# One-hot groups of an edge walk built from a row of numbers in PSUM in place of SBUF

## The reference

```python
xn = layernorm(x)
neigh_mean = segment_sum(xn[src], dst) / max(deg, 1)
gnn = normalize(relu(concat([xn, neigh_mean]) @ W + b))
mix = linear_attention(rmsnorm(xn))          # 4 heads, softmax of k over all nodes
x = x + gnn + mix
x = x + experts(layernorm(x))                # 8 experts of 256x1024x256, the best 2 of each row
```

## Time and profile before

| what | value |
|---|---|
| timed runs, median of 3 (lowest to highest) | 1980.42 us (1979.69 to 1981.53) |
| profiled execution: its span, from first to last instruction | 2187.4 us |
| time around that span | not on the page |
| PE, VectorE, ScalarE, GpSimd: busy in the span | 72%, 50%, 41%, 52% |
| the walk's first and last gather (L695) begin at | 89.5 and 1271.2 us |
| expert stage, from about 1500 us to the end: PE busy | 675 of 687 us |

### The profile page before, as it was taken

The page is one execution under the profiler, slowest core; times in us unless marked ns, Lnnn a source line. Parts: engine busy times, 40 slices in busy tenths (PEclk is TensorE's granted clock), DMA queues, the critical chain, the costliest instruction groups (busy, mean ns, idle before and its releaser), DMA issues.

```text
span 2187.4 us, 33907 instructions
## 1 busy us (share of the span) xinstructions
PE 1583.7 (72%) x9422; PEld 1361.2 (62%) x9423; DVE 1101.1 (50%) x3043; ACT 900.9 (41%) x1840; POOL 1140.4 (52%) x1141
## 2 busy tenths in 40 slices
PE   6735536546566667867767763548999999999998
PEld 5524435435454544545545543447999999999997
DVE  6512212212234536655555457765666666666664
ACT  6501101101112323323334336554666666666664
POOL 3267666666656666666666612555333333333333
PEclk9868868767878979988888785558999999999999
DMA  7334333333324655566656526537878777877775
GB/s 210 119 100 114 104 101 107 101 97 103 106 81 154 224 165 182 182 180 184 198 182 189 181 76 197 188 135 248 228 215 220 213 221 208 226 214 221 213 221 137
DMA packets 188123, 368.85 MB, mean 169 GB/s; under 512 B 33324, under 2 KB 134172, under 8 KB 173656
## 3 DMA queue, kind: packets, MB, share of 16 engines
q0 software_dynamic: 77296, 252.50, 41.3%
q1 hardware_dynamic: 102992, 113.64, 16.3%
q10 hardware_dynamic: 7736, 1.52, 0.4%
HBM read 287.94 MB, written 80.39 MB: 168 GB/s over the span
## 4 chain that ended last, share of the span: by engine, by line
PE 50%; another core or an unknown queue 17%; DVE 12%; issue 11%; DMA 5%; ACT 3%; SPq 2%; POOL 0%; DVEq 0%; ACTq 0%; POOLq 0%
PE bank L1813 11%; PE bank L2002 5%; PE bank L2003 5%; PE bank L2004 5%; PE bank L2025 5%; PE bank L2024 5%; PE bank L2026 5%; PE bank L1879 3%; DMA xTs<-xnT_d 3%; PE bank L1830 2%; PE bank L1973 1%; DVE acc_lent L1478 1%; DMA z_d<-w2s_lent 1%; DVE acc_lent L1307 1%
## 5 line engine op out<-in xcount | busy, mean ns | idle before, releaser
L695 POOL DMA_INDIRECT w2s_lent<-z_d,edge_tabs_lent x784 | 777.5, 992 | 438.7 <-issue 256.7
L1307 DVE TENSOR_TENSOR acc_lent<-acc_lent,bank 128x258 f32 x244 | 102.7, 421 | 600.6 <-remote 348.8
L1813 PE MATMUL bank<-w2s_lent,S_lent 128*128 x976 | 261.0, 416 | 19.0 <-issue 9.5
L1031 ACT ACTIVATE G<-bank,acc_lent 128x256 f32<-128x256 f32 x448 | 188.3, 472 | 205.9 <-DVE w2s L1670 124.5
L1813 PE MATMUL bank<-w2s_lent,G 128*128 x976 | 265.9, 422 | 3.4 <-issue 3.4
L2024 PE MATMUL bank<-w2s 128*128 128x256 f32 x896 | 264.4, 295 | 0.0
L2002 PE MATMUL bank<-w2s,acc 128*128 128x256 f32 x896 | 260.4, 291 | 2.8 <-issue 2.8
L739 POOL DMA_INDIRECT out_dram<-G,acc_lent x112 | 179.6, 1604 | 158.3 <-DVE G L1650 117.3
L1629 DVE TENSOR_TENSOR acc<-w1s,acc 128x512 fp32r<-128x512 f32 x224 | 155.1, 693 | 200.7 <-ACT acc L1000 174.1
L2004 PE MATMUL bank<-w2s,acc 128*128 128x256 f32 x896 | 254.0, 284 | 0.0
L2025 PE MATMUL bank<-w2s 128*128 128x256 f32 x896 | 253.7, 283 | 0.4 <-issue 0.4
(11 more groups left out here) (322 smaller groups left out, 2993.3 us busy)
## 6 DMA issues: line engine op xcount, KB each, us to landing
w2s<-w_d POOLq DMA_DIRECT2D x112, 1024.0 KB
w_d<-w2s_lent SPq DMA_DIRECT2D x64, 256.0 KB
acc_lent<-bucket_d SPq DMA_DIRECT2D x56, 266.0 KB
w2s_lent<-z_d,edge_tabs_lent POOLq DMA_INDIRECT x784
bu_d<-w2s_lent SPq DMA_DIRECT2D x98, 128.0 KB
w2s_lent<-bu_d SPq DMA_DIRECT2D x14, 768.0 KB
w1s<-in_L_ffn_W_dram SPq DMA_DIRECT2D x8, 1024.0 KB
w2s_lent<-in_L_ffn_W_dram SPq DMA_DIRECT2D x32, 256.0 KB
```

The costliest lines, as they stand in the source:

```text
L695: pool.indirect_dma_start(out=ring_rows[:, row % (RING * QUAD), 0:D], out_offset=None, in_=z_d[:, :], in_offset=bass.IndirectOffsetOnAxis( ...
L1031: g = act.activation(raw[q % 2][:, k * MT:(k + 1) * MT], bank[q][:, k * MT:(k + 1) * MT], ACT.Gelu, bias=b1c[1 - par][:, 2 * q + k:2 * q + ...
L1307: dve.tensor_tensor(to, to, bank[j % DEPTH][:, 0:ACCW], ALU.add).then_inc(s["acc_done"], 1)
L1813: m = pe.matmul(bank[j % DEPTH][:, 0:ACCW], S_of[j % DEPTH][:, k, :], rows[:, ds(bases[j], ACCW)], start=(k == 0), stop=(k == QUAD - 1))
```

## The change

Before the first builds the row of numbers is copied from SBUF into bank 6, and the builds read it there, through the first stretch of the walk. When the first half of the attention is done, which uses bank 6 afterwards, the builds go back to SBUF. After the last use of bank 5 by the context it is copied into bank 5, and read there until tile 9 of the second half, where the fold takes the bank. After tile 26 it is copied into bank 5 a third time, for the rest of the walk. The copy of b1T waits for its own end before that. All else stays.

```diff
...
+            iota_now = [iota]
+            def iota_in(b):
+                L.after(dve.tensor_copy(bank[b][:, 0:P], iota[:, :]))
+                iota_now[0] = bank[b]
             def build_S(j):
-                dve.tensor_tensor(S_of[j % DEPTH], iota[:, :].rearrange("p (o n) -> p o n", o=1).to_broadcast([P, QUAD, P]),
+                dve.tensor_tensor(S_of[j % DEPTH], iota_now[0][:, 0:P].rearrange("p (o n) -> p o n", o=1).to_broadcast([P, QUAD, P]),
                                   dstT[:, QUAD * j:QUAD * (j + 1)].rearrange("p (g o) -> p g o", o=1).to_broadcast([P, QUAD, P]),
                                   ALU.is_equal).then_inc(s["s_built"], 1)
...
+            iota_in(6)
             for j in range(DEPTH):
                 build_S(j)
...
+            iota_now[0] = iota
             kmax_tile(NT - 1, TAIL)
...
             dve.tensor_copy(M2[:, :], bank[7][:, 0:D]).then_inc(s["M2_ready"], 1)
+            iota_in(5)
...
             for t in range(NT):
                 f = t - FOLD_AT
+                if f == -1:
+                    iota_now[0] = iota
                 turn(mine[0])
...
                 if f == 2 * EXPERTS:
                     dve.wait_ge(s["b1_mm"], 1)
-                    dve.tensor_copy(b1T[:, :].rearrange("p (e c) -> p c e", c=HC),
-                                    bank[5][:, 0:HC * EXPERTS].rearrange("p (c e) -> p c e", e=EXPERTS))
+                    L.after(dve.tensor_copy(b1T[:, :].rearrange("p (e c) -> p c e", c=HC),
+                                    bank[5][:, 0:HC * EXPERTS].rearrange("p (c e) -> p c e", e=EXPERTS)))
+                    iota_in(5)
             turn(TURNS - 1)
```

## The result

| what | kernel before | changed kernel |
|---|---|---|
| timed runs, median of 11 | 1980.42 us | 1971.44 us |
| lowest to highest | 1974.43 to 1987.74 | 1965.23 to 1975.99 |
| ratio, 95% interval | | 0.9942 (0.9930 to 0.9954) |

The changed kernel is faster by 9.0 us by the medians, by 11.5 us (9.1 to 13.9) by the ratio. Forecast were 16.7 us and 1964 us.

A forecast was written before the change was run, and what follows sets the result against it. The prediction took the walk to run at GpSimd's gather pace plus a few fixed pauses. It summed 11.9 + 4.8 = 16.7 us, subtracted from the 1980.42 us median: 1964 us, range 1945 to 1978 us.

The forecast's parts named there:

- The mechanism: Walk over the edges: running builds with two SBUF inputs lengthen gathers, a bank input gives full relief; 20.6 us in 79 gathers.
- the deciding moment: Gathers in the walk: about 0.13 us from its start a gather needs something that a running build withholds.
- The build's price: VectorE's builds: nothing added to 0.684 us; the skill page's estimate was 65 ns more each, 11.9 us over 184.
- The copies: Three copies of the row on VectorE: counted as nothing, hidden under waits; without these covers 1 us, at most 1.8.
- The first stretch: First part of the walk, 94 builds: 95% of 12.5 us of lengthening arrives, 11.9 us; bounds 0 and 12.8.
- the 207 us of stalls: Profiled span beyond the timed median: if the profile adds GpSimd's pauses, lengthening counts at least as fully in timed runs.
- The second half: Two stretches of the second part, 90 builds: 60% of 8.1 us arrives, 4.8 us; bounds 0 and 8.6.
- The stalls as evidence: Walk: ScalarE's stalls of 47.84 and 24.16 us ended 3.1 and 3.9 us after GpSimd stopped, so GpSimd sets the pace.
- A: Rival, walk: builds fall anywhere in the gather's period, 55% hit a gather; 34 us gained, 1946 us; chance 0.20.
- B: Rival, walk: GpSimd's saving becomes longer waits for the ring, or a bank relieves nothing; 1980 us; chance 0.14.
- the ring: In the walk GpSimd waits for a free place in it when it is full; B had the saving become this wait.
- C: Rival, walk: without lengthenings GpSimd stops more often at a full ring; with 7 more stops 1994 us; chance 0.06.

The follow-up runs named there:

- the two kernels with doubled builds: Kernel before with every build done twice: first from SBUF, then from a bank, 1.0109, 2007.7 us; both from a bank, 1.0005, 1986.3 us.
- the profile of before: Kernel before, unchanged, run once more for a second profile: span 1978.9 us, without the long stalls; timed 1.0004, 1983.1 us.
- the stalled profile: First profile of the kernel before, unchanged, which the prediction read: span 2187.4 us, against a timed median of 1980.42 us.
- the second buffer: xTs loaded one tile earlier into one of two buffers: kernel before with it 0.9994, changed kernel 0.9910, builds from the bank in the second half alone 0.9948.
- only copies: Changed kernel's three copies of the row and their waits, all builds still from SBUF, against the kernel before: 0.9993.

## Why the prediction was right, and where it was not

*The mechanism* held. A gather waits for a running build from SBUF and not for one from a bank (0 of 60, and 32.6 us against next to nothing in the two kernels with doubled builds); the bank as first input of a full-width build does as much as the add's second. Two details were not as the prediction has them. It puts the deciding moment 0.13 us behind a gather's start; but a gather that has begun before the build is not held, even if the build begins within these 0.13 us (none of 18 in the profile of before, none of 10 in the one that the prediction read). And it found no gather held inside an add; in the sound profile of before four of 70 that began inside one are 0.15 us longer, all right behind a fold, and why isn't known. That tensor_tensor did not stall DMA, as the Trainium skill, "SBUF — State Buffer", section "Who interferes with whom", reports, does not hold for these gathers: 86 of 92 that met a build from SBUF were lengthened in the profile of before, and the other six met only the build's edge: three began within 0.03 us behind its start, and for three it ended 0.13 to 0.14 us behind theirs. What withholds what inside the chip, no run here shows. All gathers were forecast at about 757 us; they take 758.2. That is luck in part: the 20.6 us of the forecast and the 18.7 us of the profile of before lie close, but their parts, 12.5 and 8.1 against 6.9 and 11.8, do not.

*The build's price:* nothing, as forecast; 683 ns from both sources. The 65 ns that the prediction estimated from the Trainium skill's page "VectorE: DVE Perf Modes", section on the TRN2 errata, are not seen.

*The copies:* nothing, as forecast; 0.29 us each, under adds that wait for PE longer than that.

*The first stretch, the term that was mis-sized:* 12.5 us x 95% = 11.9 were forecast; 6.9 us were there, and as much arrived (6.9 us timed, 4.4 to 9.7; start of the second half 7.9 us earlier). The share was right as far as this can tell, and the 12.5 us are met in the stalled profile alone: 45 lengthened gathers in it, 28 in the next. Six sound profiles with an unchanged first stretch have 22 to 31 of them there, and 5.5 to 9.1 us. The prediction asked which way the 207 us of stalls would bend the sum and answered "at least as fully"; it did not ask whether the stalls also shift how builds and gathers fall against each other. That they do is the likely cause, but no run shows it.

*The second half, near in part by luck:* 8.1 us x 60% = 4.8 were forecast. There were 11.8 us to remove in the profile of before (9.5 to 10.8 in three others), and the half became 7.2 us shorter in the pair of profiles; timed, the change less its first stretch is 11.5 - 6.9 = 4.6 us, a difference of two measurements that are each good to some 2.5 us. So more was there than forecast, and 39% of it arrived by the timed runs, 61% by the two profiles. The reason given for the 60%, a tile's own chain nearly as slow as the gathers, is what the second buffer showed; the limiting part of it was the load of xTs in SP's queue. Alone the half gave 1.8 and 3.2 us; whether that is less than behind a shorter first stretch, the intervals don't tell. Over both parts 16.7 of 20.6 us were forecast to arrive, 81%; 11.5 of 18.7 did, 61%.

*The stalls as evidence:* the argument that GpSimd sets the pace because stalls end when it stops rests on something that no later profile contains. GpSimd does set the pace of the first part, but what shows it is some 1 us out for each 1 us taken out, and that GpSimd pauses for only 4 us in these 428 us, not the stalls.

*The rivals.* A (34 us) supposed that builds fall anywhere in the gather's period and 55% of them hit one; 64 of 184 did, 35%. B (swallowed) is what happened to part of the second half, with a load in the place of the ring: GpSimd's pauses did not grow (21 and 20 us), since a ring of eight quads let the gathers run ahead until they were done 5.4 us earlier for nothing. C (more stops) did not occur.

*Left open:* stage r took from 141.8 to 146.8 us over the sound profiles, without a visible relation to the edits (before 141.8, only copies 146.3), so a comparison of two single spans can be off by as much as 5 us here. What stalled the first profile isn't known.

## What to carry to other kernels

Where GpSimd issues indirect DMAs beside VectorE, look in the trace for gathers that end at a constant time behind a VectorE operation with two SBUF inputs; one of its operands in a bank freed them here at no price that could be seen, and a corner of a bank that is in use anyway is place enough. Before a saving on the pacing engine is counted in full, work out the period of the next chain: here a load behind a store in SP's queue made a chain nearly as long, and only shortening both paid in full. Compare a profile's span with the timed runs before its sums are used, and where it is 10% off, take a second one.

## What was not expected of the hardware

The same kernel gave a profile of 2187.4 us with stalls that have no releaser and one of 1978.9 us with none. In the sound one, VectorE's other operations with two SBUF inputs lengthen gathers as the builds do: a scalar_tensor_tensor of b_o2 (L1416) 21 gathers by 3.6 us, and a tensor_tensor (L1369) six by 3.2 us. Two inputs are not the whole condition: a CAST of 128x512 numbers with one SBUF input (L451) lengthens five of the nine gathers that met it, by 0.9 us. Stage r's spread of 5 us between profiles, far from every edit, was not expected either.
